# Key tiles 4 and 5 of the wide items' second half of P V as three fp16 products

## The reference

```python
q = hidden_states @ Wq;  k = encoder_hidden_states @ Wk;  v = encoder_hidden_states @ Wv
logits = jnp.einsum('bhqd,bhkd->bhqk', q, k) * scale
logits = logits + col_bias[None, None, :, :]      # masks on four token columns
probs = jax.nn.softmax(logits, axis=-1)
out = jnp.einsum('bhqk,bhkd->bhqd', probs, v)
out = out.transpose(0, 2, 1, 3).reshape(B, HW, HEADS * HEAD_DIM)
out = out @ Wo + bo + residual
```

## Time and profile before

| | us |
|---|---|
| median of 3 runs | 3488.54 |
| lowest, highest | 3486.07, 3488.72 |
| span of the profiled execution | 3487.1 |
| busy PE, DVE, POOL, ACT | 3363.5, 2345.2, 2182.3, 1765.5 |

### The profile page before, as it was taken

How to read it: one execution, slowest core, us unless ns; L and a number is a source line. 1 busy time by engine, 2 the same in 40 slices (tenths; PEclk the granted TensorE clock), 3 DMA queues, 4 the chain that set the end, 5 groups by cost and what they waited for, 6 DMA issues and landing times.

```text
span 3487.1 us, 70163 instructions
## 1 busy us (share of the span) xinstructions
PE 3363.5 (96%) x27442; PEld 1543.5 (44%) x27442; DVE 2345.2 (67%) x4444; ACT 1765.5 (51%) x2230; POOL 2182.3 (63%) x1050
## 2 busy tenths in 40 slices
PE   7999999999997888889999999999999999999998
PEld 3444444444442322234444444444444444444443
DVE  6666766666666788856676666666666666666666
ACT  5444444444445677764444444444444444444444
POOL 6877777767641000028777777777787677767776
PEclk9999999999998999999999999999999999999999
DMA  4000000000000000000000000000000000000000
GB/s 153 3 10 11 1 10 10 10 1 9 6 10 12 8 12 17 17 1 10 10 9 3 10 11 1 10 10 10 1 10 10 1 10 10 10 1 10 3 1 25
DMA packets 50178, 42.10 MB, mean 12 GB/s; under 512 B 4928, under 2 KB 42176, under 8 KB 49856
## 3 DMA queue, kind: packets, MB, share of 16 engines
q1 hardware_dynamic: 49136, 37.08, 3.5%
q10 hardware_dynamic: 720, 0.53, 0.1%
HBM read 32.36 MB, written 2.10 MB: 10 GB/s over the span
## 4 chain that ended last, share of the span: by engine, by line
PE 90%; ACT 3%; DVE 2%; POOL 2%; issue 2%; DMA 0%; SPq 0%; ACTq 0%; POOLq 0%; DVEq 0%
PE ps_j L858 39%; PE ps_j L1047 19%; PE ps_st L1007 13%; PE ps_sm L941 6%; PE ps_st L992 3%; PE ps_j L1034 3%; ACT pt L1495 2%; PE ps_sm L1021 2%; POOL acc L712 2%; PE ps_j L1067 1%; PE ps_st L941 1%; PE ps_j L950 1%; PE ps_j L1083 1%; PE ps_j L1058 0%; DVE nmg L1925 0%
## 5 line engine op out<-in xcount | busy, mean ns | idle before, releaser
L712 POOL TENSOR_TENSOR acc<-acc,pt 128x1024 f32<-128x1024 f32 x570 | 1365.5, 2396 | 435.8 <-ACT pt L1495 381.6
L1495 ACT ACTIVATE pt<-ps_st 128x1024 f32<-128x1024 f32 x768 | 742.7, 1019 | 447.2 <-PE ps_st L1007 435.4
L1047 PE MATMUL ps_j<-pt,v 128*64 128x512 f32 x3040 | 694.3, 599 | 1.3 <-DVE q_l L1836 1.3
L1935 DVE CUSTOM_DVE_ANT_0 ps_sm<-ps_sm,bias_m,nmx 128x512 f32<-128x512 f32 x666 | 480.5, 757 | 271.1 <-PE ps_j L941 227.5
L858 PE MATMUL ps_j<-w_h,ctx_h 128*128 128x128 f16 x3072 | 532.3, 220 | 2.3 <-ACT rinv L1511 1.1
L858 PE MATMUL ps_j<-w_l,ctx_h 128*128 128x128 f16 x3072 | 531.2, 220 | 0.0
L858 PE MATMUL ps_j<-w_h,ctx_l 128*128 128x128 f16 x3072 | 531.2, 220 | 0.0
L1935 DVE CUSTOM_DVE_ANT_0 ps_sm<-ps_sm,bias_m 128x512 f32<-128x512 f32 x486 | 334.6, 707 | 198.7 <-PE ps_j L941 185.8
L733 POOL TENSOR_TENSOR o_un<-o_un,rinv 128x512 f32<-128x512 f32 x111 | 141.7, 1277 | 477.3 <-ACT rinv L1507 293.7
L1047 PEld LDWEIGHTS ps_j<-pt,v 128*64 128x64 f32 x3040 | 201.7, 136 | 407.6 <-issue 369.6
L1972 DVE RECIPROCAL rinv<-rinv 128x256 f32<-128x256 f32 x190 | 331.4, 1746 | 14.0 <-ACT rinv L1511 4.4
(11 more groups left out here) (186 smaller groups left out, 5477.2 us busy)
## 6 DMA issues: line engine op xcount, KB each, us to landing
w_raw<-wk SPq DMA_DIRECT2D x25, 256.0 KB, 2.8
pt<-ctx_t SPq DMA_DIRECT2D x6, 1024.0 KB, 7.2
w_raw<-wv SPq DMA_DIRECT2D x24, 256.0 KB, 3.7
wo_raw<-wo SPq DMA_DIRECT2D x28, 128.0 KB, 2.0
w_raw<-wq SPq DMA_DIRECT2D x24, 128.0 KB, 2.8
k_h<-k_l SPq DMA_DIRECT2D x72, 32.0 KB, 2.0
x<-x_t SPq DMA_DIRECT2D x4, 512.0 KB, 8.3
acc<-ctx_t SPq DMA_DIRECT2D x2, 1024.0 KB, 8.4
```

What stands on the lines that cost most here:

```text
L712: G.tensor_tensor(total, first, pt[:, n % RING, :], ALU.add).then_inc(s_acc, 1)
L1047: last = MM(dst[h * HD:(h + 1) * HD, :], values_of(p)[:, kt, h * HD:(h + 1) * HD], pt[:, (units(p) + kt) % RING, h * TQ:(h + 1) * TQ], sta ...
L1495: A(pt[:, n % RING, :], src.rearrange("p h q -> p (h q)"), ACT.Exp).then_inc(s_exp, 1)
L1935: last = V.tensor_tensor_reduce(out=src, in0=src, in1=bias_m[:, t, half * HALF:(half + 1) * HALF], scale=-1.0, scalar=nmx[:, 0, t, h:h + 1 ...
```

## The change

`thirds(p)` names the items concerned: 4 to 28, 52 to 77 and 84 to 110, 78 in all. For these:

- ACT copies "v1" in two steps: key tiles 4 and 5 into fp16 `v_h`, then 6 and 7 into fp32 as before. DVE then takes the rest of 4 and 5 from PSUM (`values_lo`, into `v_l`), between its `extra_rows` and its `add_out`. PE's opening of the next slot, which takes bank 0 from "v1", now also waits for `s_v_l`.
- ACT copies P's tiles 4 and 5 to fp16 `p_h` behind exponential 5 (`weights_hi_of`), POOL takes the rests `p_l` (`weights_rest`) between additions 5 and 6.
- PE makes the second half of P V with `attend_in_thirds`: tiles 4 and 5 by three fp16 products each for both heads (12 products in place of 4 fp32 ones, which have 8 records), then tiles 6 and 7 in fp32 as before.
- `dynamic_dma_scratch_size=4096` is passed when the program is made. The rewritten condition around `keys_hi` keeps its order.

One item is treated in part: slot 29 is a `wide_slot`, which still calls `attend(28, 1)`. So item 28 gets the added copies and rests, but its second half stays in fp32, and reads for tiles 4 and 5 what an earlier item left in v32. The computation is changed there; 77 items use the new products.

PE, where slot 7 begins, before: the last products of "v1", output projection 1, then score block 0 of slot 7.

The diff, with the hunks on declarations and on `keys_hi` left out:

```diff
@@ -198,6 +198,16 @@
 def split_sums(p):
 
     return not grouped(p) and not G0 - 3 <= p < G0
+
+
+def thirds(p):
+
+    return turned(p) and all(not first - 2 <= p < first + B for first in (STARTS[layer] for layer in WIDE))
+
+
+def thirds_before(p):
+
+    return sum(thirds(q) for q in range(p))
 
 
 def splits(p):
...
@@ -711,6 +728,11 @@
                     first = total
                 G.tensor_tensor(total, first, pt[:, n % RING, :], ALU.add).then_inc(s_acc, 1)
 
+            def weights_rest(p, i):
+                n = units(p) + 4 + i
+                pool.wait_ge(s_p_h, 2 * thirds_before(p) + i + 1)
+                G.tensor_tensor(p_l[:, i, :], pt[:, n % RING, :], p_h[:, i, :], ALU.subtract).then_inc(s_p_l, 1)
+
             def sums_lo(p):
                 pool.wait_ge(s_acc_h, splits(p) + 1)
                 G.tensor_tensor(acc_l, acc[:, p % 2, :], acc_h, ALU.subtract).then_inc(s_acc_l, 1)
...
@@ -797,6 +819,9 @@
                     add(s, 5)
                     if s - STARTS[layer_of(s)] < B:
                         add_bo(layer_of(s), batch_of(s))
+                    if thirds(s):
+                        weights_rest(s, 0)
+                        weights_rest(s, 1)
                     add(s, 6)
                     add(s, 7)
                 if grouped(s + 1) and has_values(s + 1):
...
@@ -831,6 +856,8 @@
                         pe.wait_ge(s_ms_sb, m - 1)
                     elif before in ("v0", "v1"):
                         pe.wait_ge(s_v_sb, values_before(m) + 1 + int(before[1]))
+                        if before == "v1" and thirds(m):
+                            pe.wait_ge(s_v_l, thirds_before(m) + 1)
                     elif before in ("k0", "k1"):
                         pe.wait_ge(s_k_l, values_before(m) + 1 + int(before[1]))
                     elif before == "pva":
...
@@ -1047,6 +1074,24 @@
                         last = MM(dst[h * HD:(h + 1) * HD, :], values_of(p)[:, kt, h * HD:(h + 1) * HD],
                                   pt[:, (units(p) + kt) % RING, h * TQ:(h + 1) * TQ], start=k == 0, stop=k == 3)
                 last.then_inc(s_pvb if part else s_pva, 1)
+
+            def attend_in_thirds(p):
+
+                pe.wait_ge(s_exp, units(p) + 8)
+                pe.wait_ge(s_v_sb, values_before(p) + 2)
+                dst = take("pvb", p)
+                pe.wait_ge(s_v_l, thirds_before(p) + 1)
+                for i in range(2):
+                    pe.wait_ge(s_p_l, 2 * thirds_before(p) + i + 1)
+                    for n, (v, w) in enumerate(((v_h, p_h), (v_l, p_h), (v_h, p_l))):
+                        for h in range(2):
+                            MM(dst[h * HD:(h + 1) * HD, :], v[:, p % 2, i, h * HD:(h + 1) * HD],
+                               w[:, i, h * TQ:(h + 1) * TQ], start=i == 0 and n == 0, stop=False)
+                for kt in range(6, 8):
+                    for h in range(2):
+                        last = MM(dst[h * HD:(h + 1) * HD, :], values_of(p)[:, kt, h * HD:(h + 1) * HD],
+                                  pt[:, (units(p) + kt) % RING, h * TQ:(h + 1) * TQ], start=False, stop=kt == 7)
+                last.then_inc(s_pvb, 1)
 
             def sums(p):
 
...
@@ -1218,7 +1263,9 @@
                 score_block(0)
                 if far and splits_x(s):
                     project_k(s + 2, 0)
-                if past and not grouped(s - 1):
+                if past and thirds(s - 1):
+                    attend_in_thirds(s - 1)
+                elif past and not grouped(s - 1):
                     attend(s - 1, 1)
                 elif past:
                     sums(s - 1)
...
@@ -1363,7 +1410,7 @@
                 p = N - 1
                 extra_scores(p, 0)
                 turned_scores(p, 0)
-                attend(p - 1, 1)
+                attend_in_thirds(p - 1)
                 extra_scores(p, 1)
                 turned_scores(p, 1)
                 sums(p - 1)
...
@@ -1473,8 +1520,17 @@
                     act.wait_ge(s_pv, KT * (groups(p - B) + 1))
                 else:
                     reaches(act, s_pvb if half else s_pva, wides(p - 2) + 1 if p >= 2 else 0)
-                A(values_of(p)[:, half * 4:half * 4 + 4, :], bank(f"v{half}", p).rearrange("p (k d) -> p k d", k=4),
-                  ACT.Copy, scale=VS / WS).then_inc(s_v_sb, 1)
+                src, to = bank(f"v{half}", p).rearrange("p (k d) -> p k d", k=4), values_of(p)[:, half * 4:half * 4 + 4, :]
+                if thirds(p) and half:
+                    A(v_h[:, p % 2], src[:, 0:2], ACT.Copy, scale=VS / WS)
+                    src, to = src[:, 2:4], to[:, 2:4]
+                A(to, src, ACT.Copy, scale=VS / WS).then_inc(s_v_sb, 1)
+
+            def weights_hi_of(p, i):
+                n = units(p) + 4 + i
+                act.wait_ge(s_exp, n + 1)
+                reaches(act, s_pvb, wides(p))
+                A(p_h[:, i, :], pt[:, n % RING, :], ACT.Copy).then_inc(s_p_h, 1)
 
             def exponentials(p, j):
                 n = units(p) + j
...
@@ -1710,6 +1767,9 @@
                 exponentials_of(2)
                 if s % B == 0 and set_of(s) + 1 < N // B:
                     weights_hi(set_of(s) + 1)
+                if thirds(s):
+                    weights_hi_of(s, 0)
+                    weights_hi_of(s, 1)
                 first_half_out(s)
                 block_bias_out(3)
                 if nxt:
...
@@ -1916,6 +1976,11 @@
                 else:
                     split_lo(q_l[:, p % 3, :], bank("q0", p), QS, q_h[:, p % 3, :]).then_inc(s_q_l, 1)
 
+            def values_lo(p):
+                dve.wait_ge(s_v_sb, values_before(p) + 2)
+                src = bank("v1", p).rearrange("p (k d) -> p k d", k=4)
+                split_lo(v_l[:, p % 2], src[:, 0:2], VS / WS, v_h[:, p % 2]).then_inc(s_v_l, 1)
+
             def maxima(p, u):
                 dve.wait_ge(s_max_mm, units(p) + u + 1)
                 if grouped(p):
...
@@ -2125,6 +2190,8 @@
                 peak()
                 if nxt:
                     extra_rows(s + 1)
+                if thirds(s + 1):
+                    values_lo(s + 1)
                 if past:
                     add_out(s - 1, 1)
 
...
@@ -2293,7 +2360,7 @@
     arrays["wo1"] = np.ascontiguousarray(wo.reshape(n * P, C))
     arrays["norm_w"] = np.ascontiguousarray(get("L1_xattn_norm_w").reshape(CQ, P).T)
 
-    nc = bacc.Bacc("TRN2", target_bir_lowering=False, num_devices=1)
+    nc = bacc.Bacc("TRN2", target_bir_lowering=False, num_devices=1, dynamic_dma_scratch_size=4096)
     a = {k: nc.dram_tensor(k, v.shape, mybir.dt.from_np(v.dtype), kind="ExternalInput").ap()
          for k, v in arrays.items()}
     out = nc.dram_tensor("out_t", (C, B * TQ), F32, kind="ExternalOutput").ap()
```

More of the change, by code:

```diff
@@ L384, in build @@
         pt = sb("pt", [P, RING, 2 * TQ], F32)
+        p_h = sb("p_h", [P, 2, 2 * TQ], F16)
+        p_l = sb("p_l", [P, 2, 2 * TQ], F16)
+        v_h = sb("v_h", [P, 2, 2, P], F16)
+        v_l = sb("v_l", [P, 2, 2, P], F16)
         acc = sb("acc", [P, 2, 2 * TQ], F32)
@@ L460, in build @@
         s_v_sb = sem("s_v_sb")
+        s_v_l = sem("s_v_l")
+        s_p_h = sem("s_p_h")
+        s_p_l = sem("s_p_l")
         s_max_mm = sem("s_max_mm")
@@ L1702, in turned_slot @@
                     queries_hi(s + 2)
-                    if not splits_x(s):
-                        keys_hi(s + 2, 0)
+                if far and not splits_x(s):
+                    keys_hi(s + 2, 0)
+                if far:
                     keys_hi(s + 2, 1)
```

## The result

The changed kernel takes 3501.95 us (median of 4 runs, 3500.76 to 3504.26), the kernel before beside it 3488.63 (3486.07 to 3488.96). The ratio is 1.0042, with a 95% interval of 1.0028 to 1.0056: slower by 13 us, where 13.7 had been forecast. The profiled execution spans 3499.8, which is 12.7 more than before.

A forecast was written before the change was run, and what follows sets the result against it. PE, covered to 96%, was taken to bound the kernel. Terms -32.3 (products), +30.4 (values), +12.6 (slots with weights) and +3.0 (ends) made +13.7 us: span 3500.8, median 3502.2, range 3489 to 3516.

The forecast's parts named there:

- Products: PE's second half of P V: six fp16 pairs take 1.30 for 1.72, gain 0.42 per item, 32.3 us less.
- Rival 4: PE's products aren't shortened, fresh weights don't hide: a pair takes 0.31, 43 us more, about 3545; chance 0.02.
- Values: ACT's two copies, then DVE's rest, make PE's opening wait 0.39 in 78 slots, 30.4 us more.
- v: Length of the opening's wait for DVE's v_l per slot: taken as 0.39, bounds 0.25 and 0.54.
- Rivals 1 and 2: At the opening: first, no wait, 3479.6, chance 0.08; second, wait 0.03 to 0.27, about 3491 at 0.20, chance 0.19.
- Rests of P: ACT's copies and POOL's rests, 2.13 each, cost nothing in slots without weights; the sums hold by 0.45.
- rival 3: POOL's rests take 2.36, as long as additions; the 20 slots wait 1.09, about 3513; chance 0.05.
- Slots with weights: POOL's additions, lengthened beside DVE's weights split, make PE's sums wait 0.63 in 20 slots, 12.6 us more.
- the formula 1.02 - v: Sums' wait in the 20 slots with weights, as it shares slack with the opening's wait v.
- The wo split: DVE's wo split meets POOL's addition 7 in the slot after weights: taken as 0, otherwise 4 us in all.
- Ends: POOL's lateness where rows of items end: slot 78 1.2, slot 110 0.9, last slot 0.9, together 3.0 us more.
- Item 28: Costs its waits and brings no product; no sums' wait counted, since slot 29 has large slack behind it.

The follow-up runs named there:

- the kernel with the work elsewhere: Against the kernel before: key tiles 0 and 3 in three products, v_h and v_l from SBUF, POOL's rests placed separately; 3455.52 against 3488.53, ratio 0.9907.

## Why the prediction was right

The main terms and the way they add up hold, and the time with them. Three smaller things went otherwise: the last slot, what a wait costs in slot 110, and slot 28. Step by step:

- **Products.** Forecast 0.42 an item, measured 0.45 (29.58 against 30.03), in all -34.7 in place of -32.3. The six pairs take 1.32 as forecast (1.30, with the border). What they replace was a little longer than my four steps of 0.43. Rival 4 is out.
- **Values.** Forecast v = 0.39, measured 0.40, 78 times: the copies 0.38 where I had 0.39, DVE 0.43 where I had 0.42, the hand-over 0.14 as in slot 1. Together +31.2 in place of +30.4. The 0.33 that the profile shows for the wait is not the price, since a record's end lies behind the moment at which the next could have started; the distance of the slots is. The trace has this wait 78 times, as said, each 0.32 to 0.33 and ended by DVE's v_l. Rivals 1 and 2 are out.
- **Rests of P.** 2.136 each in the groups of the changed kernel (page, 156 of them, no idle time before them), as forecast, so rival 3 is out. Ordinary slots hold.

```profile
L734 POOL TENSOR_TENSOR p_l<-pt,p_h 128x1024 f16<-128x1024 f32 x156 | 330.0, 2136 | 0.0
```

- **Slots with weights.** 0.62 (30.60 against 29.98), forecast 0.63; but 19 of them, not 20. Slot 108 has no next pair of heads to split weights for, and the distance behind it is 29.98. 11.8 in place of 12.6. "In every fourth slot and in no other" is what the trace shows, but for the last of them. With v = 0 the wait is 1.02, as the formula 1.02 - v has it.
- **The wo split.** Forecast nothing, and so it is. In the slots behind those 19 DVE's split starts within an addition of POOL. The addition keeps its length, DVE's split takes 1.39 in place of 0.42, and nothing on PE hangs on it (29.98). After, then before:

```profile
202.04 4.86 POOL L729 TENSOR_TENSOR acc<-acc,pt 128x1024 f32<-128x1024 f32 x2
205.79 1.39 DVE L1896 SCALAR_TENSOR_TENSOR wo_l<-wo_raw,wo_h 128x256 f16<-128x256 f32 x1
...
207.48 0.42 DVE L1836 SCALAR_TENSOR_TENSOR wo_l<-wo_raw,wo_h 128x256 f16<-128x256 f32 x1
```

- **Ends.** Slot 78: 1.3 (30.97 to 32.31), forecast 1.2, but one step earlier than said. PE stands at the closing pair, ahead of output projection 0, for ACT's bias_m. That is queued on ACT behind the copy o_h, which waits for POOL's normalization.

```profile
2490.53 0.39 PE L968 MATMUL ps_sm<-k_h,q_h 64*128 64x512 f16 x2 [1.17 <-ACT bias_m L1631]
```

Slots 110 and 111 to the end: 2.14 + 0.45 of gain that is not seen + 0.51 = 3.1, forecast 0.9 + 0.9 = 1.8. The wait in slot 110 is 0.92 longer, as forecast, but I had taken a wait to cost its own length. At the lower clock behind it the first half of P V takes 1.68 more (before, then after):

```profile
3446.02 3.65 PE L1047 MATMUL ps_j<-pt,v 128*64 128x512 f32 x16
...
3456.99 5.33 PE L1074 MATMUL ps_j<-pt,v 128*64 128x512 f32 x16
```

The other 0.9, a wait of the last slot's sums for POOL's split, did not come: PE was late itself, and the sums start 0.31 behind the last score products, as before. The 0.51 is mostly the wait for DVE's last addition in front of the last fp32 sums, 1.45 in place of 1.01. Even with both rests left out the two sums are 27.73 apart in place of 26.03, since PE arrives earlier, waits 2.76 for the same split, and the clock falls to 0.58. A gain of PE turned there into a longer wait and a slower stretch.
- **Item 28.** Forecast nothing ("has slot 29 with its large slack behind it"), measured 3.57. I had looked at who waits for POOL's results and at POOL held up by DVE, as in the earlier trace rows, and not at DVE held up by POOL with PE behind it. That DVE can be the one who waits was in the trace of before as well, in slot 28: 256 columns of the same split, beside POOL's additions, took 2.58, where the median of its eight is 0.48.

```profile
917.44 2.58 DVE L1836 SCALAR_TENSOR_TENSOR w_l<-w_raw,norm_w_sb,w_h 128x256 f16<-128x256 f32 x1
```

- **The scratch size.** Nothing, as forecast.

With the measured terms the sum is -34.7 + 31.2 + 11.8 + 4.4 + 3.6 = +16.3. The seven stretches of the table give +16.1. The medians are 13.3 apart (by the interval, 10 to 20), and the forecast of 13.7 is near them partly by luck. Against the 16.3 it lacked 3.6 of slot 28, 1.4 of the ends and 0.8 of the values, and on the other side 2.4 of gain, and it had 0.8 too much for the slots with weights. The 3.0 between 16.3 and 13.3 are no more than what the start and the grouped items scatter by; in this pair of traces they made 3.4, with a slower clock in the start of the kernel before.

## What to carry to other kernels

When PE fills the period, the price of a split operand is paid where its PSUM bank is handed on: here the readers in series before the next writer grew from 0.74 to 1.26, and all of that beyond the slack of 0.13 was paid in every slot. The same split taken from an SBUF copy, away from the bank, cost nothing. Two waits in one period share slack, so taking out one of them alone gives less than its size; make the kernel with both out first, since it tells what there is to win (31 us here, and 36 were had by moving the work and leaving item 28 out). And before adding work to POOL, look at every DVE instruction with two SBUF inputs that will lie beside it, in both directions, above all in the few odd slots that break the pattern.

## What the hardware showed that was not expected

A wait of PE of 2 to 4 us can cost more than its length: behind the 2.27 of slot 28 the granted clock went from 1.00 to 0.55 for some 3 us and took 1.6 us more, behind the 3.22 of slot 110 it went to 0.60 and took 1.7 more, and behind 3.61 there, with the values' rest left out, it took 2.6 more. Behind waits of 2.30 (before) and 1.70 in slot 110 it stayed at 1.00, and also behind the 3.35 of slot 28 in the kernel with the work elsewhere. So the length of the wait alone doesn't decide it, and what does is open.

The port between DVE and POOL makes either of them wait: POOL's additions 1.08 longer behind DVE's split, DVE's split 1.92 longer beside POOL's rest, and DVE's split of 256 columns 0.97 longer beside an addition, 19 times, at no cost.
